# A graph network on one core: signals of TensorE joined in the three GNN passes

## The reference

```python
x = x + _L0_gnn_ref(_layernorm(x), src, dst, edge_weight, w_nbr, w_own, bias)   # one weighted graph convolution
x = x + _L0_ffn_ref(_layernorm(x)[None], ...)[0]                                # 8 experts, 2 for each node
x = x + _L1_gnn_ref(_layernorm(x), L1_gnn_W, b, gamma, beta, edge_index)         # 3 layers, below
x = x + _L1_ffn_ref(_layernorm(x)[None], ...)[0]                                # attention over 64 slices, 8 heads

def _L1_gnn_ref(x, W, b, gamma, beta, edge_index):
    row, col, norm = _gcn_norm(edge_index, n, x.dtype)     # with a self loop for each node
    for i in range(3):
        h = x @ W[i]
        h = segment_sum(h[row] * norm[:, None], col) + b[i]
        h = (h - mean(h)) * rsqrt(var(h) + 1e-5) * gamma[i] + beta[i]
        x = relu(h)
    return x
```

## Time and profile before

| | |
|---|---|
| median of three runs | 3794.12 us (3790.35 to 3794.98) |
| profiled execution, span | 4365.6 us |
| TensorE, matmuls busy | 3253.1 us, 75% of the span |
| GpSimd busy | 2531.6 us, 58% |
| VectorE busy | 1790.8 us, 41% |
| ScalarE busy | 1496.2 us, 34% |
| mean granted TensorE clock | 0.861 of full speed |
| the three passes | 2390 to 4235 us of the span |

### The profile page before, as it was taken

The page is one execution under the profiler, slowest core; times in us unless marked ns, Lnnn a source line. Parts: engine busy times, 40 slices in busy tenths (PEclk is TensorE's granted clock), DMA queues, the critical chain, the costliest instruction groups (busy, mean ns, idle before and its releaser), DMA issues. The chain is left out here.

```text
span 4365.6 us, 47498 instructions
## 1 busy us (share of the span) xinstructions
PE 3253.1 (75%) x15077; PEld 2484.5 (57%) x15077; DVE 1790.8 (41%) x5335; ACT 1496.2 (34%) x2892; POOL 2531.6 (58%) x2604
## 2 busy tenths in 40 slices
PE   1455565555446989988886798987989868999868
PEld 1344444444335777776764576655666645666547
DVE  4355565534353111111117333343333435676664
ACT  3233333323323112121115244443444434555520
POOL 6666666666643656565546666665666656666620
PEclk6677777777767999999988899988999979999978
DMA  6343334334312545554437454554544534555452
GB/s 194 111 122 109 117 115 118 116 108 120 101 40 98 176 157 179 172 185 156 157 124 269 124 146 136 149 159 116 144 138 142 166 107 143 150 153 152 135 175 103
DMA packets 396972, 609.34 MB, mean 140 GB/s; under 512 B 81648, under 2 KB 295319, under 8 KB 395943
## 3 DMA queue, kind: packets, MB, share of 16 engines
q0 software_dynamic: 115808, 279.40, 22.6%
q1 hardware_dynamic: 274182, 317.02, 22.4%
q10 hardware_dynamic: 6720, 9.74, 0.7%
HBM read 509.58 MB, written 96.33 MB: 139 GB/s over the span
## 5 line engine op out<-in xcount | busy, mean ns | idle before, releaser
L2983 POOL DMA_INDIRECT rows_h<-table,step_src x1138 | 1105.8, 972 | 688.6 <-issue 342.5
L3025 PE MATMUL bank_g<-rows_hl,counts_h 128*128 128x512 f32 x3773 | 1049.8, 422 | 89.0 <-issue 45.4
L975 POOL DMA_INDIRECT rows_r<-table,step_src x782 | 749.6, 959 | 405.2 <-issue 214.1
L3025 PEld LDWEIGHTS bank_g<-rows_hl,counts_h 128*128 128x128 f32 x3773 | 721.3, 194 | 301.9 <-issue 101.0
L1000 PE MATMUL bank_r<-rows_r,hots_r 128*128 128x257 f32 x1564 | 473.4, 457 | 457.4 <-ACT rows_r L985 227.3
L1000 PEld LDWEIGHTS bank_r<-rows_r,hots_r 128*128 128x128 f32 x1564 | 340.1, 227 | 567.6 <-ACT rows_r L985 261.6
L3184 ACT ACTIVATE counts_h<-piece_h 128x896 fp32r<-128x896 uint8 x539 | 498.1, 945 | 458.8 <-PE bank_g L3025 223.3
L1901 POOL DMA_INDIRECT kept_A<-one_d,place_d x424 | 420.7, 992 | 127.4 <-issue 127.1
L2016 PE MATMUL pY_e<-w_e,h_e 128*128 128x256 f32 x1680 | 421.7, 410 | 76.7 <-ACT h_e L1982 54.4
L1011 DVE TENSOR_SCALAR hots_r<-lane,step_dst 128x128 f32<-128x128 f32 x782 | 210.3, 289 | 593.3 <-remote 365.2
L1982 ACT ACTIVATE h_e<-pH_e,prm_e 128x256 f32<-128x256 f32 (+1 forms) x456 | 179.6, 455 | 733.7 <-PE pH_e L2005 486.5
(11 more groups left out here) (397 smaller groups left out, 3864.9 us busy)
## 6 DMA issues: line engine op xcount, KB each, us to landing
w_e<-in_L_ffn_W SPq DMA_DIRECT2D x114, 1024.0 KB
piece_h<-kept_A SPq DMA_DIRECT2D x539, 112.0 KB
kept_A<-zero_r SPq DMA_DIRECT2D x189, 112.0 KB
rows_h<-table,step_src POOLq DMA_INDIRECT x1138
table<-ACC SPq DMA_DIRECT2D x51, 256.0 KB
kept_sw<-vec_g SPq DMA_DIRECT2D x49, 256.0 KB
rows_r<-table,step_src POOLq DMA_INDIRECT x782
b_e<-in_L_ffn_b SPq DMA_DIRECT2D x57, 128.0 KB
```

Source lines behind the costliest of these rows:

```text
L975: nc.gpsimd.indirect_dma_start(out=r["rows"][:, x, 0:D], out_offset=None, in_=r["table"][:, :], in_offset=bass.IndirectOffsetOnAxis(ap=c[" ...
L2983: nc.gpsimd.indirect_dma_start(out=d["rows"][:, x, :], out_offset=None, in_=tables[l - 1][:, :], in_offset=bass.IndirectOffsetOnAxis(ap=c[ ...
L3025: mm = pe.matmul(sums, d["counts"][:, n % CV, x % PC, :], both.both(t), start=(x == 0 and i >= RINGED[l]), stop=(x == NT - 1))
```

## The change

The instructions of all engines, their operands and their order stay the same, and so do all waits of TensorE, GpSimd and SyncE. What changes is which matmul signals, and which semaphore two waits name:

- `turns` and `products`: one signal that adds `n` behind the last tile of a pair, where each tile had one that added 1.
- `lanes(l, h)`: only the first group of a pass signals `s_mm`. For the others the signal is that of `spread(l, h - 1)`, the matmul behind it; each `spread` but a pass's last now counts up `s_mm` in place of `s_spread`.
- `added` waits for `s_mm` accordingly. `s_spread` is left with one signal for each pass.
- `node_weights`: the turns no longer signal. `turned_weights` waits for the tile's sums (`s_S`), which stand behind them.

```diff
@@ turns, products (TensorE)
-                    mm.then_inc(q["T"], 1)
+                mm.then_inc(q["T"], n)
...
-                    mm.then_inc(q["M"], 1)
+                mm.then_inc(q["M"], n)
@@ lanes, spread (TensorE)
-                mm.then_inc(r["s_mm"], 1)
+                if h == 0:
+                    mm.then_inc(r["s_mm"], 1)
...
                 pe.matmul(lanes_bank(l, m)[:, 0:D], d["spread"][0:k, m % 2, :], d["mid"][0:k, m % 2, :],
-                          start=True, stop=True).then_inc(d["s_spread"], 1)
+                          start=True, stop=True).then_inc(r["s_mm"] if h < PASSES[l].GG - 1 else d["s_spread"], 1)
@@ node_weights (TensorE)
                 for a in range(PAIRS):
-                    mm = pe.transpose(pU[:, a * P:(a + 1) * P], e["sw"][u][:, a * P:(a + 1) * P], c["ident"][:, :])
-                mm.then_inc(e["s_W"], 1)
+                    pe.transpose(pU[:, a * P:(a + 1) * P], e["sw"][u][:, a * P:(a + 1) * P], c["ident"][:, :])
@@ turned_weights (ScalarE)
-                act.wait_ge(e["s_W"], o + 1)
+                act.wait_ge(e["s_S"], o + 2)
@@ added (VectorE)
-                v.wait_ge(d["s_spread"], m + 1)
+                if h < PASSES[l].GG - 1:
+                    v.wait_ge(r["s_mm"], ET + m + 2)
+                else:
+                    v.wait_ge(d["s_spread"], l)
```

## The result

The changed kernel takes **3819.7 us**, median of four runs (3818.89 to 3821.89), against 3794.55 us for the kernel before: a ratio of 1.0065, 95% interval 1.0053 to 1.0078. That is 25 us slower, where 2 us and "no change" were forecast, and outside the range of 3774 to 3812.

A forecast was written before the change was run, and what follows sets the result against it. TensorE's own stream, 85% busy in the three passes, was taken to set the pace. Terms 0 + 0 + 1.9 + 0.9 = 2.8 us on the median of 3794.12 gave 3797, written as 3796 us; range 3774 to 3812.

The forecast's parts named there:

- The signals' own price: In TensorE's stream: 285 fewer signals are worth 0 to 9.4 us, taken as 0; rival at the upper price, chance 0.15.
- the last stage's remainder: Last stage, 392 records with 49 signals: 1.6 us unexplained, at most 0.033 us a signal if all due to signals.
- Turns and products: ScalarE's wait for a pair's tiles: it waits for all of them before and now, so cost 0.
- Lanes and spread: Group signal to VectorE and GpSimd: 0.63 us later, 140 times, hidden in their idle time; cost 0 within a pass.
- Turned weights: ScalarE's copy of a tile's turned weights: 1.73 us later, absorbed by ScalarE's next idle stretch; cost 0 within the pass.
- Ends of passes: At each pass's end no next group hides the group signal's 0.63 us: 1.9 us lost in all.
- the last store: End of the last pass: the last copy and its store move later, costing 0 to 1.7 us, taken as 0.9.
- The slower rival: Pass 3: late turned weights hold up ScalarE's conversions, 15 TensorE waits each growing 1.73 us, 26 us lost, 3823; chance 0.14.
- the prediction's own sign: TensorE's waits for counts_h in pass 3: growth from 27.9 us by 20 or more would show the prediction wrong.
- The other sign: TensorE's idle time in the passes, 277 us, should stay the same within 10 us.
- A rival on late signals: In the passes, TensorE's signals are seen late and fewer relieve it: at most 66 us, credibly 3772 to 3787; chance 0.13.

The follow-up runs named there:

- e7_signals_back: The changed kernel with 189 signals put back on a semaphore that nobody waits for, waits still late: 3818.3 us, 1.0063 of the kernel before.
- e1_pairs: The kernel before with only the signals of turns and products joined (96 fewer): ratio 0.9998 to the kernel before.
- e9_groups_12: The kernel before with only the group signals of lanes moved behind spread, in passes 1 and 2 alone: ratio 1.0003 to the kernel before.
- the second profile: A repeat profile of the kernel before, nothing changed: 3790.8 us measured, span 3788.7 us, against 4365.6 us in the first profile.
- the single parts: Two runs on the kernel before: only the group signals moved, 1.0031 (12 us slower), and only the turned weights' wait moved, 1.0045 (17 us slower).

## Why the prediction was wrong

**The signals' own price, 0 of a possible 9.4 us: right.** The four turns of L2996 still take 0.60 us with one signal in place of two, and `e7_signals_back` shows no cost of 189 signals added. The upper bound, drawn from the last stage's remainder, was no price of signals. The 7.5 us that the prediction estimated from the Trainium skill, TensorE: Matmul & The Clock Gate, section "The cost: per-tile semaphore tail", did not come either. No run here shows a gain from fewer increments, though a few us would be within the intervals.

**Turns and products, 0: right within 4 us** (`e1_pairs`).

**Lanes and spread, 0 within a pass: right in passes 1 and 2, wrong in pass 3.** The step that failed reads: "VectorE had stood still for 580.7 us in 106 waits, 5.5 us each. 0.63 us fits in." A mean over three passes was used for a stage that is different. In pass 3 VectorE is busy for 411.7 of 587.7 us (70%), against 42% in the passes before, and 105.8 us of waiting for the groups are left in 32 waits for 53 groups: 21 groups had none. More than that, who waits behind VectorE was not followed on: `kept` stands ahead of a softmax step, the softmax step ahead of ScalarE's exponential, and that ahead of a conversion. Measured: 12 us, where 0 was put down.

**Turned weights, 0 within the pass: wrong.** The step was: "So what shifts is absorbed by the next idle stretch." It was read off ScalarE's row at 3693.44 and its share of about 50%. It looked at one place, where ScalarE next waits for TensorE and the delay does vanish. At other places the next idle stretch is a wait for VectorE, and that wait ends as much later as ScalarE itself was late with the root. ScalarE's extra waiting was sized well, up to 57 us forecast and 66 us found; that it is hidden was the error. Measured: 17 us.

**The clock was in no term.** The sum counts only time that TensorE stands still. About half of what was lost in the stretch of 2296 records, 10.5 of 21.2 us, is busy time that grew because the granted clock fell behind some of the stops.

**Ends of passes, 1.9 us, and the last store, 0.9 us: not settled.** Two of the three ends are in `e9_groups_12`, whose interval is wider than their 1.3 us, and what follows pass 3 differs by 1 to 5 us between executions with the same waits.

**The slower rival had the right sign and one of the right places; its size was luck.** It named conversions held up in pass 3, 15 waits growing by 1.73 us, 3823 us against 3819.7 measured. In fact the waits for counts are 7 in the second profile, and they grew by 5.3 us in sum, not by 26. The rest of the loss is other waits behind late copies of ScalarE, and the slower clock. About 70% of it stays when the conversions are taken out from behind the exponentials, and 12 of the single parts' 29 us come from the groups, which it did not name. By the prediction's own sign, counts growing by 20 us or more, this rival would have been missed. The other sign was good: TensorE's idle time in the three passes grew from 109.5 to 124.3 us, by more than the 10 allowed. The rival got a chance of 0.14, and the range stopped at two thirds of it.

**Reading a doubtful profile.** The 15% between profiled span and median was noted and then only used to doubt waits. It also made pass 3 look looser than it is: TensorE busy for 549.89 of its 635 us, 87%, where the second profile has 541.67 of 587.7, 92%. A rival on late signals (0.13) was built on rows that only that execution has.

## What to carry to other kernels

Joining a signal with a later one is free only if everything that waits for it has slack, and idle time before a wait is no proof of that: follow what the engine waits for one step further, since two engines that hand work to and fro both look idle. Do this in the stage with the highest shares, not with a mean over stages. And look at what stands in the queue right behind a wait: here work that nothing in the softmax needed, a conversion, was placed behind an exponential, and moving the exponential gained 12 us in the kernel before, where the joins gained nothing. When an experiment takes one route of a loss away, compare what is left as well: here the most visible wait carried the smaller part.

## What the runs showed of the hardware

A matmul's signal cost nothing that could be measured in TensorE's stream, also when it adds two (0.9998 with 96 signals joined in pairs).

In a stream that is nearly full, a slightly longer stop can cost more than its length, because the granted clock falls behind it. With a stop of 1.21 us in front, four matmuls of L3081 took 1.98 us; with one of 2.33 us, the same four took 3.59. Over a stretch of 2296 matmul records, 10.7 us more of standing still came with 10.5 us more of busy time, at a mean granted clock of 0.98 against 1.00. Which stops bring the clock down was not worked out.
